# Output projection once per block of four tiles, with 512 columns, in a windowed-attention transformer kernel

## The reference

```
def attn_layer(x, Wqkv, qs, ksc, Wo):
    qkv = x @ Wqkv
    ...                                   # l2norm, rotary, windows
    out = local_attention(q, k, v)
    out = out.transpose(0, 2, 1, 3).reshape(b, n, INNER)
    return out @ Wo                        # INNER = 1024 -> 128
...
x = attn_layer(shift_tokens(x), Wqkv[i], q_scale[i], k_scale[i], Wo[i]) + x
x = ffn_layer(shift_tokens(x), ln_g[i], ln_b[i], W1[i], b1[i], W2[i], b2[i]) + x
```

## Time and profile before

| | |
|---|---|
| median of 3 runs | 3262.96 us (3260.38 to 3264.7) |
| profiled execution, its own time | 3261.53 us |
| its span | 3259.2 us |
| mean granted TensorE clock | 0.99 of full speed |
| busy: PE, weight loads | 3196.7 us (98%), 2554.4 us (78%) |
| busy: DVE, ACT, POOL | 82%, 75%, 68% |

### The profile page before, as it was taken

How to read it: one execution, slowest core, us unless ns; L and a number is a source line. 1 busy time by engine, 2 the same in 40 slices (tenths; PEclk the granted TensorE clock), 3 DMA queues, 4 the chain that set the end, 5 groups by cost and what they waited for, 6 DMA issues and landing times.

```text
span 3259.2 us, 149853 instructions
## 1 busy us (share of the span) xinstructions
PE 3196.7 (98%) x62709; PEld 2554.4 (78%) x62709; DVE 2656.8 (82%) x6367; ACT 2431.3 (75%) x5028; POOL 2215.8 (68%) x1332
## 2 busy tenths in 40 slices
PE   8889999999999999999999999999999999999997
PEld 6768778878877877887887787787788778778875
DVE  6678888878888888887888888888788888888884
ACT  3348777777777777777777778777777777877774
POOL 5558767767767776776776776676677677767762
PEclk9989999999999999999999999999999999999998
DMA  4521111122111131211122111122111122112111
GB/s 161 193 102 50 47 42 47 53 87 61 44 43 45 51 94 48 56 44 41 49 84 60 53 48 43 42 82 69 48 49 43 43 65 88 50 45 54 49 45 37
DMA packets 110574, 200.00 MB, mean 61 GB/s; under 512 B 19280, under 2 KB 40784, under 8 KB 109136
## 3 DMA queue, kind: packets, MB, share of 16 engines
q1 hardware_dynamic: 107168, 185.17, 19.7%
q10 hardware_dynamic: 2736, 5.25, 0.5%
HBM read 41.45 MB, written 23.07 MB: 20 GB/s over the span
## 4 chain that ended last, share of the span: by engine, by line
PE 92%; DMA 0%; ACT 0%; issue 0%; DVE 0%; SPq 0%; ACTq 0%; DVEq 0%
PE psum L797 25%; PE psum L881 12%; PE psum L822 12%; PE psum L897 12%; PE psum L834 7%; PE psum L855 5%; PE psum L842 5%; PE psum L957 4%; PE psum L942 4%; PE psum L947 4%; PE psum L926 1%; PE psum L908 1%; DMA xsh<-xs_in 0%; PE psum L917 0%; DMA ff_x<-x_mid 0%
## 5 line engine op out<-in xcount | busy, mean ns | idle before, releaser
L443 POOL TENSOR_TENSOR qks<-work 128x1024 f32<-128x1024 f32 x384 | 910.7, 2372 | 134.9 <-issue 125.4
L451 POOL TENSOR_TENSOR qkr<-qks,rnorm 128x1024 f32<-128x1024 f32 x384 | 732.2, 1907 | 307.9 <-issue 221.6
L797 PE MATMUL psum<-wparts,xhi 128*128 128x512 f32 x2304 | 821.5, 438 | 10.1 <-POOL xlo L428 5.1
L577 ACT ACTIVATE sq<-psum 128x512 f32<-128x512 f32 x768 | 459.8, 599 | 302.4 <-PE psum L797 281.5
L459 POOL TENSOR_TENSOR probn<-prob,psumr 128x512 f32<-128x512 f32 x384 | 402.0, 1047 | 369.2 <-DVE psumr L1188 369.2
L1137 DVE TENSOR_REDUCE ssq<-sq 128x8 f32<-128x512 f32 x768 | 517.5, 674 | 3.5 <-ACT sq L577 3.4
L1164 DVE TENSOR_TENSOR work<-psum,rot 128x512 f32<-128x512 f32 x768 | 506.9, 660 | 2.0 <-POOL qks L443 1.8
L822 PEld LDWEIGHTS psum<-kT,qTs 64*32 64x32 f32 x24576 | 360.9, 107 | 144.5 <-issue 129.8
L797 PEld LDWEIGHTS psum<-wparts,xhi 128*128 128x128 f32 x2304 | 384.4, 190 | 99.3 <-issue 45.8
L797 PE MATMUL psum<-wparts,xlo 128*128 128x512 f32 x1152 | 459.4, 399 | 0.0
L1182 DVE TENSOR_REDUCE psumr<-prob 128x8 f32<-128x512 f32 x384 | 261.3, 680 | 242.4 <-ACT prob L629 239.5
(11 more groups left out here) (139 smaller groups left out, 5584.0 us busy)
## 6 DMA issues: line engine op xcount, KB each, us to landing
vsh<-vtok SPq DMA_DIRECT2D x384, 192.0 KB, 2.4
vsh<-vtok SPq DMA_DIRECT2D x384, 64.0 KB, 2.5
wsplit<-wstage SPq DMA_DIRECT2D x15, 1024.0 KB, 6.3
wparts<-wsplit SPq DMA_DIRECT2D x30, 512.0 KB, 4.3
xsh<-xs_in SPq DMA_DIRECT2D x192, 64.0 KB, 2.8
ff_x<-x_mid SPq DMA_DIRECT2D x96, 128.0 KB, 2.4
wraw<-Wqkv_dram SPq DMA_DIRECT2D x18, 512.0 KB, 4.1
rsplit<-rstage SPq DMA_DIRECT2D x5, 1024.0 KB, 4.0
```

Source lines behind the costliest of these rows:

```text
L443: pool.tensor_tensor(qks[:, :, :], rcos, rsin, ALU.add).then_inc(s["add_ready"], 1)
L451: pool.tensor_tensor(qkr[:, n % 2, :, :], qks[:, :, :], rnorm[:, :].unsqueeze(2).to_broadcast([P, 2 * OCT, DH]), ALU.mult).then_inc(s["qkr ...
L577: act.activation(sq[:, w * OCT:(w + 1) * OCT, :], bank[w].rearrange("p (h n) -> p h n", n=DH), ACT.Square).then_inc(s[("sqq_ready", "sqk_r ...
L797: mm = pe.matmul(out, xparts[xp][:, ti, :], wparts[:, SECTION_AT[w, oc], wp_, :], start=(k == 0), stop=(k == 2))
```

## The change

`output` and `residual` run once per block of four tiles in place of once per tile. aoT grows from two tiles to four, so that it gathers the block's attention output; each of the eight matmuls then has 512 columns (four tiles) and fills bank 5. That happens in step 5 of a block (`step % 8`), 48 times in place of 192. All counts of wo_ready and x_mid_ready follow: the wait of `attended` before it overwrites aoT, of the value projection before it overwrites bank 5, of the fetch of x for the FFN, and of the reload of Wo.

```
-        aoT = sb("aoT", [P, 2, HEADS // 2, P])
+        aoT = sb("aoT", [P, TPI, HEADS // 2, P])
...
-                sp.wait_ge(s["wo_ready"], layer * TILES)
+                sp.wait_ge(s["wo_ready"], layer * BLOCKS)
...
-                need(sp, "x_mid_ready", b * TPI + TPI)
+                need(sp, "x_mid_ready", b + 1)
...
             def attended(n):
-                tp, oc = n // UPT % 2, n % UPT
+                t, oc = n // UPT % TPI, n % UPT
                 need(act, "pv_ready", n + 1)
-                need(act, "wo_ready", n // UPT - 1)
+                need(act, "wo_ready", n // UNROLL)
...
-                if n % 2:
-                    need(pe, "x_mid_ready", (n - 4 + 1) // UPT)
+                if n % UNROLL == 3:
+                    need(pe, "x_mid_ready", n // UNROLL)
...
             def output(n):
-                if not is_unit(n) or n % UPT == 0:
+                if not is_unit(n) or n % UNROLL < UNROLL - 1:
                     return
-                tp, tile = n // UPT % 2, n // UPT
+                b = n // UNROLL
                 need(pe, "aot_ready", n + 1)
                 need(pe, "vs_ready", min(n + 4, STEPS))
-                need(pe, "x_mid_ready", tile)
+                need(pe, "x_mid_ready", b)
...
                 for k in range(HEADS // 2):
-                    mm = pe.matmul(bank[5][:, 0:P], wo[:, k, :], aoT[:, tp, k, :],
+                    mm = pe.matmul(bank[5].rearrange("p (t n) -> p t n", t=TPI), wo[:, k, :], aoT[:, :, k, :],
                                    start=(k == 0), stop=(k == HEADS // 2 - 1))
...
             def residual(n):
-                if not is_unit(n) or n % UPT == 0:
+                if not is_unit(n) or n % UNROLL < UNROLL - 1:
                     return
...
-                need(dve, "wo_ready", n // UPT + 1)
-                dve.tensor_tensor(x_mid[:, col + 1:col + 1 + P], bank[5][:, 0:P], xs_in[:, col + HIST:col + HIST + P],
-                                  ALU.add).then_inc(s["x_mid_ready"], 1)
+                b = n // UNROLL
+                col = b % BLOCKS * BLK + b % BLOCKS // 2 + 1
+                need(dve, "wo_ready", b + 1)
+                dve.tensor_tensor(x_mid[:, col:col + BLK], bank[5], xs_in[:, col:col + BLK], ALU.add).then_inc(s["x_mid_ready"], 1)
```

More of the change, by code:

```diff
@@ L546, in attended @@
                     return
-                tp, oc = n // UPT % 2, n % UPT
+                t, oc = n // UPT % TPI, n % UPT
                 need(act, "pv_ready", n + 1)
-                need(act, "wo_ready", n // UPT - 1)
-                act.activation(aoT[:, tp, oc * PAIRS:(oc + 1) * PAIRS, :].rearrange("p a (h n) -> p a h n", h=2),
+                need(act, "wo_ready", n // UNROLL)
+                act.activation(aoT[:, t, oc * PAIRS:(oc + 1) * PAIRS, :].rearrange("p a (h n) -> p a h n", h=2),
                                psum[:, 6:8, 0:256].rearrange("p h (a n) -> p a h n", n=64), ACT.Copy).then_inc(s["aot_ready"], 1)
@@ L887, in output @@
             def output(n):
-                if not is_unit(n) or n % UPT == 0:
+                if not is_unit(n) or n % UNROLL < UNROLL - 1:
                     return
-                tp, tile = n // UPT % 2, n // UPT
+                b = n // UNROLL
                 need(pe, "aot_ready", n + 1)
                 need(pe, "vs_ready", min(n + 4, STEPS))
-                need(pe, "x_mid_ready", tile)
-                if tile % TILES == 0:
-                    pe.wait_ge(s["wo_in"], tile // TILES * 16 + 16)
+                need(pe, "x_mid_ready", b)
+                if b % BLOCKS == 0:
+                    pe.wait_ge(s["wo_in"], b // BLOCKS * 16 + 16)
                 for k in range(HEADS // 2):
-                    mm = pe.matmul(bank[5][:, 0:P], wo[:, k, :], aoT[:, tp, k, :],
+                    mm = pe.matmul(bank[5].rearrange("p (t n) -> p t n", t=TPI), wo[:, k, :], aoT[:, :, k, :],
                                    start=(k == 0), stop=(k == HEADS // 2 - 1))
@@ L1168, in residual @@
             def residual(n):
-                if not is_unit(n) or n % UPT == 0:
+                if not is_unit(n) or n % UNROLL < UNROLL - 1:
                     return
-                tile = n // UPT % TILES
-                col = tile * P + tile // TPB
-                need(dve, "wo_ready", n // UPT + 1)
-                dve.tensor_tensor(x_mid[:, col + 1:col + 1 + P], bank[5][:, 0:P], xs_in[:, col + HIST:col + HIST + P],
-                                  ALU.add).then_inc(s["x_mid_ready"], 1)
+                b = n // UNROLL
+                col = b % BLOCKS * BLK + b % BLOCKS // 2 + 1
+                need(dve, "wo_ready", b + 1)
+                dve.tensor_tensor(x_mid[:, col:col + BLK], bank[5], xs_in[:, col:col + BLK], ALU.add).then_inc(s["x_mid_ready"], 1)
             def probability_sum(n):
```

## The result

The changed kernel took 3362.31 us (median of 4 runs, 3360.5 to 3363.77) against 3261.74 us of the kernel before in the same measurement: a ratio of 1.0311, 95% interval 1.0298 to 1.0324, so 100.6 us slower. The forecast was 3344 (82 slower), in a range of 3300 to 3368.

A forecast was written before the change was run, and what follows sets the result against it. PE was taken to bound the loop, waiting for nobody. PE's saving -12.5, start of step 0 +42, step 2 +34, step 3 +16, tail +3: +82 us, so 3344 us, range 3300 to 3368.

The forecast's parts named there:

- The bound, and where the loss comes: In the loop PE bounds; its work falls 0.26 us a block (-12.5 us), but lost cover makes it wait for feeders.
- Step 7 to 0: Start of step 0: `projection` waits for POOL's xlo, 0.88 us each time, +42 us.
- Step 2: DVE's FFN statistics and norm make PE late into step 3: 0.75 us in 46 blocks, +34 us.
- the two waits that were forecast: In step 2, `turn_probabilities` waits for `ffn_normed` (0.19 us); step 3's `projection` waits for DVE's q rotation.
- Step 3: Gate matmuls begin earlier, so L947 waits for ACT's first gelu: 0.35 us, 46 times, +16 us.
- The stretch: The 7 us output at the end of step 5: ACT's `attended` waits for it, costed at nothing, at most 0.6.
- The tail: The last output and residual, hidden by nothing, grow while earlier outputs leave PE's chain: +3 us.
- B: Rival: only the wait for x is real, steps 2 and 3 run as before; 3296, up to 3305 us; chance 0.15.
- C: Rival: the stretch is not covered, ACT restarts late and step 6 loses up to 0.6 us; 3373 us; chance 0.10.
- D: Rival: PE's waits bring the clock down once a block, 38 to 77 us more, about 3400; chance 0.05.
- E: Rival: wide output matmuls are as cheap as the skill's ratio says, some 225 us in all; chance 0.01.
- A: Rival: faster, the saved PE time is all that happens; 3250 us; chance 0.04.

The follow-up runs named there:

- e7: Changed kernel with ACT making xhi one step earlier and SP issuing x's fetch two steps earlier: 3318.76 us, ratio 1.0171.
- e6: As e2, but DVE's four FFN norm operations are one over 512 columns, computing other values: 3339.89 us, ratio 1.0233.
- e2: Changed kernel, but in step 2 ACT turns k before it waits for DVE's statistics (`ffn_inverse`): 3366.35 us, ratio 1.0319.
- e10: Changed kernel with the edits of e7 and e2, and the up projection's second half after step 4's q projection: 3310.96 us, ratio 1.0146.
- e3: Changed kernel, output still once per block but as 32 matmuls of 128 columns in place of 8 of 512: 3387.42 us, ratio 1.038.
- e8: As e4, with e7's edits and the up projection's second half after step 4's q projection: 3258.34 us, ratio 0.9987.
- e4: Changed kernel, but output and residual once per two tiles, 256 columns, at the end of steps 1 and 5: 3323.63 us, ratio 1.0187.

## Why the prediction was right, and where it was off

- **The bound, and where the loss comes.** Right. By the table PE's own work is 0.29 us a block less (forecast 0.26), though that column is reckoned with the forecast's own openings; measured are the 5.08 by which step 5 to 6 grew, as forecast. The rest is waits for feeders in steps whose output had been covering them. No other engine has become the bound over the block; each wait belongs to one step.
- **Step 7 to 0.** 0.89 against 0.88, released by POOL's xlo as said. xhi and xlo of that step after, from the timeline of ACT and POOL:

```profile
1542.83 0.41 ACT L570 ACTIVATE xhi<-xsh 128x256 fp32r<-128x256 f32 x1
...
1543.32 0.73 POOL L428 TENSOR_TENSOR xlo<-xsh,xhi 128x256 fp32r<-128x256 f32 x1 [0.73 <-ACT xhi L570]
```

  xlo ends at 1544.05, PE starts at 1544.10, the handoff of rows 5. Shown by taking it away (some 36 of e7's 45 us).
- **Step 2.** Right in its bound (e6: one to one; e2: the two waits that were forecast, at 0.3 us each), too small in size: 1.04, not 0.75, 14 us over 46 blocks. The step that failed is "less the residual at 1581.22 that is no longer there". DVE's step 2 is as long without it, 8.33 us (1555.06 to 1563.39) against 8.30 (1576.85 to 1585.15), because another wait was under it:

```profile
1557.59 1.36 DVE L1224 TENSOR_SCALAR ff_x<-psum,fmv,frstd 128x128 f32<-128x128 f32 x4
1558.86 0.68 DVE L1137 TENSOR_REDUCE ssq<-sq 128x8 f32<-128x512 f32 x1
1559.63 0.18 DVE L1146 TENSOR_REDUCE ssg<-ssq 128x16 f32<-128x32 f32 x1
```

  L1146 reads what L1137 writes and starts 0.77 after it, 0.09 after its recorded end, while independent operations follow at 0.60. The residual (0.19) had stood in that gap. The Trainium skill (Perfetto Trace Analysis, section "DVE / Act Engine Instruction (TENSOR_ADD, Activation, etc)") says that the recorded end is when the write is acknowledged, and that the semaphore is visible to others only after it; the 0.09 us here agree. The remaining 0.1 is the handoff: PE starts 0.14 after DVE's next operation (1563.39 to 1563.53), where 0.04 was taken. The ordering of ACT's queue, `k_turned` behind `ffn_inverse`, was missed as a wait: 25.9 us in the view of waits, worth nothing by e2.
- **Step 3.** Right in its place, 0.49 against 0.35, but the mechanism was only half of it. The wait for gelu, the one forecast, costs 0.22: the first record of L947 starts 0.55 after the last of L942 and the next one 0.53 after it, 0.43 being usual. The other 0.25 is PE's wait for `attended` inside L942 (0.61 and 0.50 in place of 0.43), which the prediction put at nothing; before, the third gate record started 1.75 us after ACT was done there, behind the output. So the term for gelu was too high (0.35 for 0.22), the missing one made up for it, and that the sum came near is in part luck. Both waits can be had back (e10: 11.04).
- **The stretch.** Costed at nothing, and it cost nothing, though ACT waits 6.9 us a block for it and not some 5.
- **The tail.** By the sum of the terms 48 x -0.29 + 48 x 0.89 + 46 x 1.04 + 46 x 0.49 = +99 us, the tail has 1 or 2 of the 100.6 us, not 3. From the last scores record to the end the profile after has 53.0 us and that of before 49.5, 3.5 more, but the last blocks' share of the other terms is in it; its parts were not separated.
- **The size.** 18 us too low: 14 from step 2, 6 from step 3, less some 2 from the other terms. With all bounds low the prediction's terms add up to 3296 and not 3290, with all high to 3374 and not 3378; the range doesn't hang on it.
- **The rivals.** B (only x) is out by e10. C by step 6. D by the clock of 1.00 with 2.1 us of waits in every block; that such falls do come in this loop, e3 shows. E, the ratio of the Trainium skill (TensorE: Matmul & The Clock Gate, section "Back-to-back issue gap") for 128 and 512 columns, by e3: 13 us between the two widths over the whole run, where that ratio gives 225. The 1% that the prediction gives under E is not in its rows: a record of 128 columns takes (1.98 - 0.19) / 16 = 0.112 us there, and four of them are 4% more than one of 512 (0.43); e3 measured 4% too. A: e8 shows what is left of it when every cover is replaced, 0.13 us a block.

## What to carry to other kernels

When one engine is the bound and never waits, any work taken out of its queue shortens the time its neighbours have at exactly that place: before moving it, list for each step what must arrive by its end, and at which time after the step's start it arrives now. Where the work stands can matter more than how cheap it is: here one output at the end of step 1, ahead of DVE's norm, was worth 1.0 us a block (e4 against the changed kernel), and four times the width 0.28 (e3). An idle that a view puts down to no engine can be a wait all the same (`attended` in step 3): compare the starts of single records with before. And a wait in the view of waits has a price only if nothing else stands behind it within its length: take it away before counting it.

## What the runs showed of the hardware that was not expected

- At f32, with a 128x128 weight tile, the time for the same columns in all hardly depends on the width from 128 to 512: 355.7 us for 3072 records of 128 columns, 342.3 for 768 of 512, in one group each (e3 and the changed kernel). With 256 columns, in e8's 96 groups of 16, it is 357.1.
- A DVE operation with two scalars per partition over 128x512 from PSUM took 0.80 us (e6), while scaling from SBUF by one column (L1254, before) took 0.45.
- A wait of 1.9 us on PE was not always followed by the lower clock. Before, the granted clock was 0.50 (1.2 GHz) right behind the 1.88 us wait of the fill; in the changed kernel the same wait was followed by 1.00 (the lines below), and the 1.84 us wait in e3's loop again by a fall. What decides between them these runs don't show, and so the prediction's reading under D, that this gap brings the clock down, holds for the one trace it was read from:

```profile
234.76 0.73 PE L797 MATMUL psum<-wparts,xhi 128*128 128x512 f32 x2 [1.87 <-POOL xlo L428]
```

```profile
236.00:238.00 2.00, 2.00 (x64) 1.78 (x53) 1.58 (x3) 1.27 (x4) 1.92 (x2) 1.00 0.04 8
```
